# A layer of causal attention and gated routed experts on one core: pair tables in the first stage, routing half a period earlier, mask and row maximum in one pass

## The reference

```python
xn = layernorm(x)                               # over the 256 features
q, k, v = xn @ WQ, xn @ WK, xn @ WV
s = softmax(causal(q @ k.T / 16)) @ v           # per batch of 512
scores = softmax(xf @ w_gate.T)                 # xf: xn as (4096, 256); 8 experts
masked = scores + expert_bias, kept in the two best of four groups of two experts
topk_idx = top_k(masked, 2)                     # 2 experts for each token
weights = scores at topk_idx
counts = bincount(topk_idx)
flat_idx = topk_idx.reshape(-1)
routed_in = xf[flat_idx] * weights
h = silu(grouped_mm(routed_in, w1, counts)) * grouped_mm(routed_in, w3, counts)
routed_out = grouped_mm(h, w2, counts)
shared = silu(xf @ sw1.T) * (xf @ sw3.T) @ sw2.T
out = x + s * silu(shared.at[flat_idx].add(routed_out))
```

## Time and profile before

| | us |
|---|---|
| median of 3 runs | 238.85 |
| lowest and highest run | 238.68, 239.2 |
| the profiled execution | 240.62 |
| its span, first to last instruction | 238.6 |

### The profile page before, as it was taken

One profiled execution on the slowest core, in us unless ns is written; L12 is line 12 of the kernel. 1 busy time (PEld: TensorE's weight loads), 2 busy tenths in 40 slices (PEclk: granted clock), 3 DMA queues, 4 the chain that ended last, 5 costly groups with the idle time before them and its releaser, 6 DMA issues.

```text
span 238.6 us, 4677 instructions
## 1 busy us (share of the span) xinstructions
PE 230.6 (97%) x1533; PEld 205.8 (86%) x1533; DVE 186.8 (78%) x620; ACT 144.9 (61%) x392; POOL 55.4 (23%) x108
## 2 busy tenths in 40 slices
PE   7898999999999999999999999999999999999983
PEld 5788998998989989999899998898988889898843
DVE  3779859989899899897977985677776867869765
ACT  2444745755648457474574723779678696878722
POOL 5220631805509136073012000002020201202000
PEclk9999999999999999999999979999999999999999
DMA  5699420020200200000000000116847557393523
GB/s 156 207 326 304 157 91 1 1 87 5 88 3 0 88 3 3 0 3 0 0 3 1 0 3 0 48 26 196 142 105 197 76 145 122 103 199 57 140 74 102
DMA packets 18758, 19.45 MB, mean 82 GB/s; under 512 B 1064, under 2 KB 17712, under 8 KB 18736
## 3 DMA queue, kind: packets, MB, share of 16 engines
q1 hardware_dynamic: 15568, 16.02, 21.4%
q0 software_dynamic: 3168, 3.15, 9.1%
HBM read 14.95 MB, written 4.21 MB: 80 GB/s over the span
## 4 chain that ended last, share of the span: by engine, by line
PE 92%; DMA 2%; DVE 2%; ACT 1%; issue 1%; SPq 1%; DVEq 0%; ACTq 0%
PE bank L392 85%; PE bank L484 4%; PE bank L440 3%; DMA raw_qkv<-in_L_attn_WK 2%; DVE raw_sw L1382 1%; DVE w L1380 1%; PE bank L556 1%; PE bank L414 0%; SPq L220 0%; DVE arena L949 0%; ACT xT_hi_all L731 0%; ACT arena L731 0%; ACT probs L731 0%; ACT attn_all L731 0%; SPq L222 0%
## 5 line engine op out<-in xcount | busy, mean ns | idle before, releaser
L392 PE MATMUL bank<-xT_hi_all,arena 128*128 128x512 f32 (+3 forms) x256 | 80.7, 370 | 0.7 <-DVE arena L949 0.7
L392 PE MATMUL bank<-arena 128*128 128x256 f32 (+2 forms) x560 | 76.8, 285 | 0.3 <-ACT attn_all L731 0.3
L392 PEld LDWEIGHTS bank<-arena 128*128 128x128 f32 (+1 forms) x560 | 71.9, 186 | 5.0 <-issue 0.8
L392 PEld LDWEIGHTS bank<-xT_hi_all,arena 128*128 128x128 f32 x256 | 47.0, 189 | 8.3 <-ACT probs L761 1.4
L731 ACT ACTIVATE arena<-bank 128x512 fp32r<-128x512 f32 (+4 forms) x84 | 36.2, 452 | 24.4 <-PE bank L392 23.1
L949 DVE TENSOR_TENSOR arena<-bank,arena 128x264 fp32r<-128x264 f32 (+4 forms) x83 | 41.4, 508 | 6.9 <-ACT arena L731 6.0
L392 PE MATMUL bank<-xT_lo_all,arena 128*128 128x512 f32 (+3 forms) x128 | 45.8, 358 | 0.0
L383 POOL DMA_DIRECT2D x_ring<-in_L_attn_x x6 | 7.9, 1317 | 79.0 <-DVE x_ring L1318 79.0
L392 PEld LDWEIGHTS bank<-xT_lo_all,arena 128*128 128x128 f32 x128 | 24.2, 189 | 2.1
L731 ACT ACTIVATE attn_all<-bank,row_inv 128x256 f32<-128x256 f32 x32 | 15.2, 474 | 17.3 <-PE bank L392 15.5
L761 ACT ACTIVATE probs<-bank,neg_max 128x128 f32<-128x128 f32 (+3 forms) x32 | 17.0, 530 | 12.6 <-DVE neg_max L1008 12.5
(11 more groups left out here) (128 smaller groups left out, 381.9 us busy)
## 6 DMA issues: line engine op xcount, KB each, us to landing
x_ring<-in_L_attn_x SPq DMA_DIRECT2D x7, 512.0 KB, 3.5
x_ring<-in_L_attn_x POOLq DMA_DIRECT2D x6, 512.0 KB, 6.0
out<-x_ring SPq DMA_DIRECT2D x6, 512.0 KB, 3.3
spread<-pairs SPq DMA_DIRECT2D x14, 128.0 KB, 3.3
w_sb<-in_L_ffn_w SPq DMA_DIRECT2D x1, 1024.0 KB, 11.9
raw_sw<-in_L_ffn_sw SPq DMA_DIRECT2D x3, 256.0 KB, 4.2
x_ring<-in_L_attn_x SPq DMA_DIRECT2D x2, 256.0 KB, 2.9
xn<-in_L_attn_x SPq DMA_DIRECT2D x1, 512.0 KB, 5.3
```

The lines of the kernel that those rows point to most:

```text
L392: return nc.tensor.matmul(dst, lhsT, rhs, start=start, stop=stop, skip_group_check=True, **kw)
```

## The change

Three parts.

**Tables.** They are made in steps b = 2 to 5 of the first stage, with the 8 tokens stationary (high and low parts side by side: 16 columns, `first8`) and the expert weights moving (256 columns, high and low part). ACT makes the high part of 512 columns of weights (`table_high`, two in a step), POOL the low part (`table_low`, two), TensorE does 8 matmuls (`tables`), ACT keeps the 16 rows (`table_keep`), SP sends them to DRAM in two transfers and, when all four are there, brings both tables back in three. POOL adds the halves and splits A.

**Routing.** In step 6 DVE does all of batch 5's instructions and 12 of batch 6's, in step 7 the other 8 and 9 of batch 7's. TensorE does all four `hidden` of the first batch, and the count after them, then one `hidden` of the next. `weigh(7, 3)` moves behind the first `hidden`.

**Mask and maximum.** The mask has 512 columns; one `tensor_tensor_reduce` adds it to the whole row, negates, writes the row back and takes the minimum. ACT's exponential has scale -1.

At the end the sums are multiplied by table B before the turn, which was done behind it.

Some of the diff (functions that are only moved, semaphore names and the buffers' definitions are left out, and most of DVE's order):

```diff
+        def table_weights(k):
+
+            return w13[:, k // 4, 2 * (k % 4):2 * (k % 4) + 2, :, :].rearrange("p e c h -> p (e c h)")
...
-            for b in range(1, LOOP1):
+            for b in range(1, TABLES + 1):
                 step(b)
+
+            for b in range(TABLES, LOOP1):
+                n, e4 = (b - TABLES) // 2, 4 * ((b - TABLES) % 2)
+                if b + 1 < LOOP1:
+                    step(b + 1)
+                sp.wait_ge(s["tables_kept"], b - TABLES + 1)
+                for h in range(2):
+                    sp.dma_start(tables_dram[n, e4:e4 + 4, :, h, :].rearrange("g j d -> j g d"),
+                                 table_cols[8 * h:8 * h + 8, :, :]).then_inc(s["tables_out"], 16)
+            sp.wait_ge(s["tables_out"], 16 * 8)
+            sp.wait_ge(s["xn_done"], B - 1)
+            for rows in (slice(0, PAIRS), slice(PAIRS, P)):
+                sp.dma_start(A_halves[rows, :, :], tables_dram[0, :, :, :, :].rearrange("g j h d -> (g j) h d")).then_inc(s["tables_back"], 16)
+            sp.dma_start(B_halves, tables_dram[1, :, :, :, :].rearrange("g j h d -> (g j) h d")).then_inc(s["tables_back"], 16)
...
+                if TABLES <= b + 1 < TABLES + 4:
+                    table_low(2 * (b + 1 - TABLES))
+                    table_low(2 * (b + 1 - TABLES) + 1)
...
+            pool.wait_ge(s["tables_back"], 16 * 3)
+            pool.wait_ge(s["scored"], 3 * (B - 1))
+            nc.gpsimd.tensor_tensor(B_rows[:, :], B_halves[:, 0, :], B_halves[:, 1, :], ALU.add
+                                    ).then_inc(s["b_ready"], 1)
+            pool.wait_ge(s["b_ready"], 1)
+            nc.gpsimd.tensor_tensor(A_sum[:, :], A_halves[:, 0, :], A_halves[:, 1, :], ALU.add).then_inc(s["a_summed"], 1)
+            pool.wait_ge(s["a_hi"], 1)
+            nc.gpsimd.tensor_tensor(A_stack[PAIRS:P, :], A_sum[PAIRS:P, :], A_stack[PAIRS:P, :].bitcast(F32), ALU.subtract
+                                    ).then_inc(s["a_ready"], 1)
+            pool.wait_ge(s["a_ready"], 1)
...
+                if t == 0 and TABLES < b <= TABLES + 4:
+                    pe.wait_ge(s["tables_kept"], b - TABLES)
...
+            def tables(n):
+                pe.wait_ge(s["first8_ready"], 2)
+                pe.wait_ge(s["v_lo"], T * (n + TABLES + 1))
+                for u in range(2):
+                    pe.wait_ge(s["table_lo"], 2 * n + u + 1)
+                    w = w_split[:, u, :, :].rearrange("p h (e c d) -> p h e c d", e=2, c=C)
+                    for c in range(C):
+                        for h in range(2):
+                            ins = mm(v_bank[0:16, u * D:(u + 1) * D], first8[:, c, :], w[:, h, :, c, :], c == 0 and h == 0, c == C - 1 and h == 1)
+                ins.then_inc(s["tables_summed"], 1)
...
                 turn_probs(b, 0)
+                if TABLES <= b < TABLES + 4:
+                    tables(b - TABLES)
                 scores(b, 2)
                 scores(b, 3)
                 turn_probs(b, 1)
```

TensorE's last attention step and what follows it:

```diff
             turn_probs(b, 1)
             scores(b, 3)
             turn_sw(2)
-            table(0, 0)
             weigh(b, 0)
             turn_probs(b, 2)
-            table(0, 1)
             weigh(b, 1)
             turn_probs(b, 3)
-            table(0, 2)
             weigh(b, 2)
-            table(0, 3)
-            weigh(b, 3)
...
-            pe.wait_ge(s["a_split"], 2)
-            nc.tensor.transpose(x_bank[0][:, 0:P], A_T[:, :].bitcast(F32), ident[:, :]).then_inc(s["a_turned"], 1)
-            table(1, 0)
             pe.wait_ge(s["sw_ready"], 3)
             pe.wait_ge(s["exp_done"], T * B)
             hidden(0, 0, 0, h1_bank, "h1_done")
-            table(1, 1)
-
-
+            weigh(b, 3)
+
+            hidden(0, 1, 0, h1_bank, "h1_done")
+            pe.wait_ge(s["pT_lo"], T * B)
+            hidden(0, 0, 1, h3_bank, "h3_done")
+            hidden(0, 1, 1, h3_bank, "h3_done")
             pe.wait_ge(s["route"], ROUTED)
             for n in range(4):
                 ins = mm(bc_bank[:, 0:P], ones_bf[:, :], at_least[:, :, :, :].rearrange("p t k e -> p (t k e)")[:, n * P:(n + 1) * P],
                          n == 0, n == 3)
             ins.then_inc(s["counted"], 1)
-            pe.wait_ge(s["pT_lo"], T * B)
-            hidden(0, 0, 1, h3_bank, "h3_done")
-            table(1, 2)
+            hidden(1, 0, 0, h1_bank, "h1_done")
             pe.wait_ge(s["rows_ready"], 1)
             turn_pairs()
             spread_pairs(0)
-            hidden(0, 1, 0, h1_bank, "h1_done")
             pe.wait_ge(s["a_ready"], 1)
             gather(0, 0)
             spread_pairs(1)
+            gather(0, 1)
             pe.wait_ge(s["pairs_kept"], 1)
-            table(1, 3)
-            hidden(0, 1, 1, h3_bank, "h3_done")
-            gather(0, 1)
             pe.wait_ge(s["attn_kept"], T * B)
-            pe.wait_ge(s["b_kept"], 1)
             mm(acc_bank[0:PAIRS, 0:2 * H], zero_bf[:, 0:PAIRS], zero_bf[:, 0:2 * H], True, True)
...
             def step2(i):
-                hidden(i, 0, 0, h1_bank, "h1_done")
+                if i > 1:
+                    hidden(i, 0, 0, h1_bank, "h1_done")
                 hidden(i, 0, 1, h3_bank, "h3_done")
                 shared_out(i - 1, 0)
                 accumulate(i - 1, 0)
```

ACT:

```diff
+            def table_high(n, u):
+                if n == 0 and u == 0:
+                    act.wait_ge(s["experts_loaded"], 16 * 6)
+                if n > 0:
+                    act.wait_ge(s["tables_summed"], n)
+                copy(w_split[:, u, 0, :], table_weights(2 * n + u)).then_inc(s["table_hi"], 1)
+
+            def table_keep(n):
+                act.wait_ge(s["tables_summed"], n + 1)
+                if n > 0:
+                    act.wait_ge(s["tables_out"], 16 * 2 * n)
+                copy(table_cols.rearrange("p e d -> p (e d)"), v_bank[0:16, :]).then_inc(s["tables_kept"], 1)
...
                 exp_logits(b)
+                if TABLES <= b < TABLES + 4:
+                    table_keep(b - TABLES)
                 v_high(p, 0)
...
                 p_high(b, 3)
+                if b == B - 2:
+                    act.wait_ge(s["a_summed"], 1)
+                    copy(A_stack[:, :], A_sum[:, :]).then_inc(s["a_hi"], 1)
+                if TABLES <= b + 1 < TABLES + 4:
+                    table_high(b + 1 - TABLES, 0)
                 keep_attn(b, 2)
                 v_high(p, 3)
+                if TABLES <= b + 1 < TABLES + 4:
+                    table_high(b + 1 - TABLES, 1)
                 keep_attn(b, 3)
...
             keep_attn(b, 2)
-            act.wait_ge(s["tables_summed"], 4)
-            copy(A_T[:, 0:PAIRS], x_bank[0][:, 0:PAIRS]).then_inc(s["a_split"], 1)
             keep_attn(b, 3)
-            act.wait_ge(s["a_turned"], 1)
-            copy(A_stack, x_bank[0][:, 0:P]).then_inc(s["a_ready"], 1)
...
             silu_hidden(0, 0)
+            silu_hidden(0, 1)
+            h_high(0, 0)
             act.wait_ge(s["pairs_turned"], 1)
             copy(pair_T[:, :], acc_bank[0:NR, 3 * P:4 * P]).then_inc(s["pairs_kept"], 1)
-            h_high(0, 0)
             silu_rows(0, 0)
-            silu_hidden(0, 1)
             rows_high(0, 0)
+            h_high(0, 1)
             silu_rows(0, 1)
-            h_high(0, 1)
             rows_high(0, 1)
```

DVE:

```diff
             def row_max(b, i):
                 dve.wait_ge(s["scores_done"], T * b + i + 1)
-                last = sc_bank[i % 2][:, i * P:(i + 1) * P]
-                nc.vector.tensor_tensor(last, last, causal_bf[:, :], ALU.add).then_inc(s["masked"], 1)
-                dve.wait_ge(s["masked"], T * b + i + 1)
-                nc.vector.tensor_reduce(neg_max[:, i:i + 1], sc_bank[i % 2][:, 0:(i + 1) * P], AX.X, ALU.max,
-                                        negate=True).then_inc(s["max_done"], 1)
+                n = (i + 1) * P
+                row = sc_bank[i % 2][:, 0:n]
+                nc.vector.tensor_tensor_reduce(out=row, in0=row, in1=causal_wide[:, S - n:S], scale=-1.0, scalar=-MASKED,
+                                               op0=ALU.add, op1=ALU.min, accum_out=neg_max[:, i:i + 1]).then_inc(s["max_done"], 1)
...
+            b = B - 2
+            p = b + 1
...
+            routes(b - 1, 17, 18)
+            v_low(p, 1)
+            routes(b - 1, 18, 20)
+            p_low(b, 2)
+            routes(b, 0, 2)
+            q_low(p, 0)
+            routes(b, 2, 3)
+            invert(b, 2)
+            v_low(p, 2)
+            routes(b, 3, 4)
+            p_low(b, 3)
+            routes(b, 4, 6)
+            invert(b, 3)
+            routes(b, 6, 7)
+            q_low(p, 1)
+            routes(b, 7, 8)
+            v_low(p, 3)
+            routes(b, 8, 12)
...
+            routes(b - 1, 18, 19)
             p_low(b, 1)
-            also(8)
+            routes(b - 1, 19, 20)
             row_max(b, 3)
-            also(9)
+            routes(b, 0, 1)
             sw_low(1)
-            also(10)
+            routes(b, 1, 2)
             invert(b, 2)
-            also(11, 12, 13, 14)
```

(25 more changed lines are left out.)

161 lines of the change are left out of this document (89 added, 72 removed).

## The result

The changed kernel takes **241.5 us** (median of 4 executions, 241.1 to 242.22); the kernel before, alongside, 239.02 us (4, 238.68 to 239.24). The ratio is 1.0103, with a 95% interval of 1.0081 to 1.0125: slower by 2.5 us. The forecast was 241.4. The experiments show that the match is luck in part: two errors of about the same size cancelled.

The account below looks back on a forecast made before the run. TensorE, busy 97% of the span, was taken to bound the kernel. Terms 4.0 + 0.1 - 2.65 + 0.3 + 0.8 = +2.55 us on 238.85 gave 241.4 us, range 238.1 to 243.6.

Parts of the forecast that it names:

- last sums to the turn: End of the kernel: the product with table B stands between reduce and turn, with one more wait, +0.3 us.
- Part 1, tables: Steps 2 to 5: 8 added TensorE matmuls a step at 0.126 us each, +4.0 us in all.
- the lower bound from the 8-column records: Table matmuls in steps 2 to 5, priced from old 8-column table records at 0.10 us each: 3.2 us.
- ACT's two copies and POOL's subtractions: Weight preparation for the tables in the first stage: ACT's copies +0.1 us, POOL's subtractions nothing.
- Part 2, the fused pass in steps 0 to 6: DVE saves an add of 0.29 us a block, but TensorE doesn't wait for it: no gain.
- Part 3, the last step: Last attention step to shared_out(0, 0): removed tables leave waits, ACT's chain gains 0.55 us, in all -2.65 us.
- The clock: New waits in the last step and behind the count make TensorE's clock fall once: +0.8 us.
- the rival without a fall: All terms the same but no fall of TensorE's clock: 240.6 us, chance 0.20.
- From the span to the median: The median lay 1.8 us below the profiled execution of 240.62; the same difference was applied, giving 238.85 as base.
- ACT's chain forward: At weigh(7, 1) and weigh(7, 2), ACT's chain comes forward as far as TensorE: 2.8 us gained, 238.3 us; chance 0.16.
- The fused pass isn't shorter: Fused mask and maximum takes as long as the two passes, chain gains 0: 242.0 us; chance 0.12, shared.
- POOL holds up DVE: Start of steps 2 to 5: POOL's subtractions delay DVE's first maximum, its sign, +2.0 us, 243.4; chance 0.12, shared.

Follow-up runs that it names:

- experiment 1: The kernel before, unchanged, run for more executions and a second profile: 238.89 us, ratio 0.9998.
- experiment 5: The changed kernel without any of the work that makes tables A and B in the first stage: 237.68 us, ratio 0.9956 to the kernel before.
- experiment 2: The kernel before with only the one-pass mask and maximum added: 237.5 us, ratio 0.9924.
- experiment 3: The changed kernel with mask and maximum in two passes again: 242.93 us, ratio 1.0161 to the kernel before.
- experiment 4: The kernel before without the 16 matmuls of table A's quarters in the last attention step: 240.95 us, ratio 1.0056.
- experiment 6: The changed kernel with three first-batch hidden calls moved ahead of weigh(7, 1), weigh(7, 2) and weigh(7, 3): 239.54 us, ratio 1.0018 to the kernel before.
- experiment 8: The changed kernel with hidden calls moved into TensorE's waits both in the last attention step and behind the count: 238.47 us, ratio 0.9976 to the kernel before.
- 9: The changed kernel with both fillings of hidden calls, and ACT's first two SiLU instructions moved between copies of the last attention rows: 237.08 us.
- 10: The kernel of 9 with ACT's and DVE's sequence 1 work on hidden activations moved earlier in the second stage: 235.55 us, ratio 0.9828 to the kernel before.
- Experiment 7: The changed kernel with three second-batch hidden calls moved ahead of gather(0, 0), gather(0, 1) and shared_out(0, 0): 239.9 us, ratio 1.0045 to the kernel before.

## Why the prediction was right, and where not

The total was right, through two errors of about the same size, and that it is right to 0.1 us is luck. The table sets the terms against two executions of the kernel before: the forecast was made on the first one, which had the fall of the clock; experiment 1 is what most executions look like. Each number is a difference of two distances in PE's timelines, after less before.

| stretch | forecast | against the first | against experiment 1 |
|---|---|---|---|
| start of the first step | 0 | +0.05 | +0.34 |
| steps 0 to 6 (108.04 and 108.02 before, 110.51 after) | +4.1 | +2.47 | +2.49 |
| last step to `shared_out(0, 0)` (29.95 and 28.41, 27.58) | -2.65, and most of +0.8 | -2.37 | -0.83 |
| from there to the last sums (67.76 twice, 68.01) | the rest of +0.8 | +0.25 | +0.25 |
| last sums to the turn (3.09 and 3.10, 3.48) | +0.3 | +0.39 | +0.38 |
| the rest | 0 | -0.09 | -0.03 |
| span | +2.55 | +0.7 | +2.6 |

**Part 1, tables: right.** 0.125 us for each of the 8 matmuls, 1.00 a step and 4.0 in all, as taken from the earlier trace rows; steps 0 to 6 grew by 3.69 against the same kernel without them (110.51 against 106.82, experiment 5), and by only 2.49 against the kernel before, since the fused pass took out 1.20 at the same time (part 2); the lower bound from the 8-column records was not needed. ACT's two copies and POOL's subtractions cost TensorE nothing that a step shows: +0.1 forecast; steps 2 to 5 are 0.91 longer for 1.00 us of matmuls, and show no sign of it. Of the missing 0.09 us one place gives 0.07: the first matmul of `scores(4, 2)` is followed after 0.19 us here (84.79 to 84.98), and after 0.26 in experiment 5 (83.27 to 83.53), where it stands right behind the turn.

**Part 2, the fused pass in steps 0 to 6: wrong.** "In steps 0 to 6 TensorE doesn't wait for it, so the gain is nothing" is the step that failed. TensorE did wait, about 0.2 us in each step (0.1 in step 6), ahead of `scores(b, 3)`, as the pair of matmuls in experiments 1 and 2 shows (0.76 against 0.57 us); neither a bracket nor a sum of idle time does. The gain is 1.2 us without the tables (experiment 1 to 2: 108.02 to 106.82) and 0.63 beside them (3 to the changed kernel). It could have been read: in the earlier trace rows I looked at the end of a step only, and the distances between starts of equal matmuls would have given it.

**Part 3, the last step: the mechanism right, the baseline wrong.** The quarters did fill waits (experiment 4), the waits came where they were expected: 1.15 and 1.14 us for the two of "about 1.2", 0.51 for 0.65, 0.94 for 1.0, 1.15 for 1.25. The chain came forward by 0.76 us (`weigh(7, 2)` 9.99 us into its step, against 10.75 in both executions of before) instead of 0.55. But 8.19 us from `weigh(7, 2)` to the count held a fall of the clock that most executions don't have; in those it is 6.65, and the change is worth 1.5 us less. Part of the gain that was booked for the last step was the fall that the first execution had.

**The clock: right, and cheaper than its full length.** One fall, from about 153.9 to 157.3, behind the wait of 1.15 us. Its price comes from experiment 6, which has the same instructions there at full clock: `gather(0, 1)` to `shared_out(0, 0)` took 2.99 us (151.97 to 154.96), here 3.56; and 2.00 to the next gather, here 2.14. That is 0.57 + 0.14 = 0.7, forecast 0.8. All four executions of the changed kernel have a mean granted clock of 0.986 to 0.993, while 55 of 66 of the one before are at 0.997 or more; no execution of it shows the rival without a fall. The falls go with the waits: all 22 executions of the changed kernel and of experiments 3 and 5, which have all five waits, are at 0.993 or lower, and all 24 of experiments 8, 9 and 10, where most are filled, at 0.996 or higher. The Trainium skill ("TensorE: Matmul & The Clock Gate", "Why this matters for your kernels") lets the clock drop only behind a far longer gap. The traces of the changed kernel and of experiment 3 disagree with it: there no wait from the last attention step to the fall is longer than 1.15 and 1.71 us.

**From the span to the median: wrong.** "The median of the runs is 1.8 us below that execution; I put the same difference on it" took the difference for a property of profiling. It was that one execution's clock: the changed kernel's profiled execution (241.42) is at its median (241.5). This makes the forecast 1.8 us too low: the gain of part 3 was read against an execution with the fall, and then put on a median without it. It is one error with the baseline of part 3, not a second one. Against it stand the steps, forecast 1.6 us too dear (1.2 for the fused pass of part 2, 0.4 in the tables' terms), and the two cancel: 240.62 + 2.55 = 243.2 would have been the forecast without the first. Taken from an execution like experiment 1, the same terms would have been 4.1 - 1.1 + 0.3 + 0.8 = 4.1 us (243.0), 1.5 too many, and the 1.6 us of the steps account for all of it.

**The rivals.** *ACT's chain forward* fell: `weigh(7, 1)` waited 1.15 us. *The fused pass isn't shorter* fell: by the medians of experiments 2 and 3 it is worth 1.4 us. *POOL holds up DVE* happens, and the sign that the prediction named for it is there, but it costs TensorE nothing. Timeline of POOL at the start of step 4 of the changed kernel:

```profile
81.28 2.53 POOL L399 TENSOR_TENSOR arena<-w,arena 128x512 fp32r<-128x512 f32 x2
```

and of DVE:

```profile
81.38 1.26 DVE L1103 TENSOR_TENSOR raw_qkv<-gs 128x64 f32<-128x64 f32 x1
82.57 0.29 DVE L1064 CUSTOM_DVE_ANT_0 bank<-bank,causal_wide 128x128 f32<-128x128 f32 x1
...
82.78 1.12 DVE L1103 TENSOR_TENSOR raw_qkv<-gs 128x64 f32<-128x64 f32 x1
```

Two choice instructions, 0.2 us each elsewhere, last about as long as POOL's two (1.27 each), and the mask between them, which reads PSUM, keeps its 0.29. The Trainium skill ("SBUF — State Buffer", "Who interferes with whom") says so, and this trace agrees. The first maximum of a step does move back: it starts 1.03 us into step 4 (81.54 to 82.57), against 0.82 in experiment 5, whose step 4 begins at 81.02 and has no work of POOL there:

```profile
81.84 0.30 DVE L1039 CUSTOM_DVE_ANT_0 bank<-bank,causal_wide 128x128 f32<-128x128 f32 x1 [0.77 <-PE bank L425]
```

But `turn_probs(b, 0)` on TensorE, which needs it, starts 2.23 us into the step here (83.77) and 2.22 there (83.24). The second maximum starts 2.87 us into the step instead of 1.98; what needs it, `scores(b, 3)`, stands behind the 1.00 us of `tables`, and steps 2 to 5 are 0.91 us longer for that 1.00. So the cost is nothing as long as the tables' matmuls cover it.

**Where the expected gain of the move went.** Work was moved from a place where half of it, table A's quarters, cost TensorE nothing (experiment 4), to one where it costs 3.8 us (experiment 5). For table B's quarters no run shows it alone. That experiment 5, which makes no table at all, isn't faster than experiment 2, which makes both in the old places (237.68 and 237.5 us), points the same way, but experiment 5 has falls of the clock in it. What was left behind were waits. Filling them in TensorE's order alone gives back 3.0 us (experiment 8), and two reorderings on ACT and DVE 2.9 more (9 and 10). What stays open: why the clock falls behind these waits in some executions and not in others, as in experiment 4. Experiment 7 left waits of 1.15, 1.14 and 1.63 us, and its profiled execution has a clock of 1.00 throughout, so the length of one wait doesn't decide it; no run separates the wait from the kind of work around it.

## What to carry to other kernels

Before moving work off the engine that bounds a kernel, ask what that engine would do in its place: if the work stands where it waits for another engine's chain, taking it away only shows the wait, and it pays only together with other work that is ready to go there. To find short waits in TensorE's queue (0.2 us here) compare distances between starts of like instructions, since the records overlap and no idle time is shown. And look at the granted clock of the profiled execution against several others before a fall in it is booked as part of the kernel, or as part of the profiler's cost.
